# A narrow attention layer prepared by the layer ahead of it, and narrow layers that project one batch before their first scores

## What is computed

```python
x = x + tanh(g_xattn[0]) * L0_xattn(layernorm(x), ctx_768, ...)     # L0x: 16 heads of 8, biases, clipped scores
x = x + tanh(g_ffn[0])   * L0_ffn(layernorm(x), ...)                # butterfly transforms; weights "L0w"
...                                                                # L1x, L1f, L2x: heads of 64, experts
x = x + tanh(g_ffn[2])   * L2_ffn(layernorm(x), ...)                # L2f: ends in (y - mu) * rsqrt(var) * ln_g + ln_b
x = x + tanh(g_xattn[3]) * L3_xattn(layernorm(x), ctx_768, mask, Wq, Wk, Wv, Wo)   # L3x: no biases, a key mask
x = x + tanh(g_ffn[3])   * L3_ffn(layernorm(x), ...)

def attention(x, context):          # per batch b of 8, per head h of 16
    q, k, v = x @ Wq, context @ Wk, context @ Wv      # x: 256x128, context: 512x96
    p = softmax(q_h @ k_h.T * 8 ** -0.5)              # 256x512
    return concat_h(p @ v_h) @ Wo
```

## Time and profile before

| | |
|---|---|
| median of three runs | 1991.5 us (1983.24 to 1994.39) |
| the profiled execution's own time | 1993.19 us |
| its span, first to last instruction | 1991.4 us |
| L0x, block start to first row scores | 14.7 to 38.5 us |
| L0x, first exponential | 56.4 us |
| L2f ends, L3x begins | 1589.8, 1590.05 us |
| L3x, first row scores | 1614.6 us |
| L3x, first exponential | 1628.4 us |

### The profile page before, as it was taken

How to read it: one execution, slowest core, us unless ns; L and a number is a source line. 1 busy time by engine, 2 the same in 40 slices (tenths; PEclk the granted TensorE clock), 3 DMA queues, 4 the chain that set the end, 5 groups by cost and what they waited for, 6 DMA issues and landing times. The chain is left out here.

```text
span 1991.4 us, 42094 instructions
## 1 busy us (share of the span) xinstructions
PE 1743.8 (88%) x16392; PEld 1016.1 (51%) x16392; DVE 1283.0 (64%) x2318; ACT 1014.8 (51%) x1944; POOL 1062.2 (53%) x1436
## 2 busy tenths in 40 slices
PE   6899988969999999967957999999987799999335
PEld 2344333636666666645743666666654434444323
DVE  4899996566766666625446567666634558886571
ACT  1555544426666666645534666666652337766101
POOL 2388981127777787754034788888884021110026
PEclk9899999869999999988987999999997899999557
DMA  6411100300111111107010011111010022220302
GB/s 185 188 41 43 49 25 1 79 23 2 27 27 27 27 27 23 23 7 219 24 34 13 3 26 27 27 27 27 23 23 17 8 76 63 59 53 10 89 14 29
DMA packets 95687, 85.45 MB, mean 43 GB/s; under 512 B 13382, under 2 KB 85186, under 8 KB 95461
## 3 DMA queue, kind: packets, MB, share of 16 engines
q1 hardware_dynamic: 88481, 68.48, 13.3%
q10 hardware_dynamic: 3172, 10.10, 1.3%
q0 software_dynamic: 3840, 4.20, 1.2%
HBM read 65.74 MB, written 17.54 MB: 42 GB/s over the span
## 5 line engine op out<-in xcount | busy, mean ns | idle before, releaser
L1150 DVE TENSOR_REDUCE L2x_neg_max<-L2x_row_ps 128x2 f32<-128x1024 f32 x128 | 156.6, 1223 | 123.8 <-PE L2x_row_ps L976 123.6
L1150 DVE TENSOR_REDUCE L1x_neg_max<-L1x_row_ps 128x2 f32<-128x1016 f32 x128 | 155.6, 1216 | 121.4 <-PE L1x_row_ps L976 121.2
L757 POOL TENSOR_TENSOR L1x_fold<-L1x_probs 128x512 f32<-128x512 f32 x128 | 172.1, 1344 | 72.4 <-ACT L1x_probs L844 66.4
L363 ACT ACTIVATE L0x_probs<-L0x_st_ps 128x512 f32<-128x512 f32 x256 | 139.0, 595 | 130.0 <-PE L0x_st_ps L438 111.0
L757 POOL TENSOR_TENSOR L2x_fold<-L2x_probs 128x512 f32<-128x512 f32 x128 | 171.0, 1336 | 62.1 <-ACT L2x_probs L844 54.5
L844 ACT ACTIVATE L1x_probs<-L1x_st_ps 128x512 f32<-128x512 f32 x256 | 139.0, 595 | 93.2 <-PE L1x_st_ps L990 84.2
L844 ACT ACTIVATE L2x_probs<-L2x_st_ps 128x512 f32<-128x512 f32 x256 | 139.0, 595 | 92.9 <-PE L2x_st_ps L990 83.0
L363 ACT ACTIVATE L3x_probs<-L3x_st_ps 128x512 f32<-128x512 f32 x256 | 139.2, 597 | 63.2 <-PE L3x_st_ps L438 63.1
L562 DVE TENSOR_REDUCE L3x_neg_max<-L3x_row_ps 128x2 f32<-128x1024 f32 x128 | 155.4, 1219 | 19.0 <-PE L3x_row_ps L427 18.3
L562 DVE TENSOR_REDUCE L0x_neg_max<-L0x_row_ps 128x2 f32<-128x1024 f32 x128 | 155.0, 1214 | 12.7 <-PE L0x_row_ps L427 11.9
L1008 PE MATMUL L1x_u_ps<-L1x_probs,L1x_vst 128*64 128x256 f32 x1024 | 124.6, 385 | 1.2 <-ACT L1x_probs L844 1.2
(11 more groups left out here) (629 smaller groups left out, 4773.5 us busy)
## 6 DMA issues: line engine op xcount, KB each, us to landing
L1x_r_wide<-scratch_r SPq DMA_DIRECT2D x14, 512.0 KB, 6.7
L2x_r_wide<-scratch_r SPq DMA_DIRECT2D x14, 512.0 KB, 6.3
L0w_up<-in_L_ffn_up_weights ACTq DMA_DIRECT2D x9, 512.0 KB
L0w_down<-in_L_ffn_down_weights ACTq DMA_DIRECT2D x9, 512.0 KB
L0x_kst<-scratch_L0x_k SPq DMA_DIRECT2D x8, 512.0 KB, 4.1
L3x_kst<-scratch_L3x_k SPq DMA_DIRECT2D x8, 512.0 KB, 4.2
scratch_L0x_k<-L0x_k_hi SPq DMA_DIRECT2D x16, 128.0 KB, 2.3
L0x_qst<-scratch_L0x_q SPq DMA_DIRECT2D x8, 256.0 KB, 2.7
```

The costliest lines, as they stand in the source:

```text
L363: act.activation(probs[n % PROBS][:, 2 * half:2 * half + 2, :], st_ps[half][:, :, :], ACT.Exp, scale=sh.scale).then_inc(exp_ready, 1)
L757: pool.tensor_tensor(fold[:, :, :], pr[:, 0:2, :], pr[:, 2:4, :], ALU.add).then_inc(fold_step, 1)
L1150: dve.tensor_reduce(neg_max[k % 4][:, t, r % 2, :], row_ps[:, :, 0:sh.keys], AXX, ALU.max, negate=True)\
```

## The change

Two things are done.

For L3x, a new object `NarrowAhead` holds its weights, the contexts of batches 0 and 1 and its statistics in SBUF, outside both layers. L2f's SyncE stream issues the loads behind its own; L2f's VectorE computes statistics of tiles 0 to 3 in the middle of its last loop and ScalarE their two activations at the end; L2f's TensorE adds 24 filling products at its end. In L3x the seven loads, the 24 filling products and the wait for `preset` on TensorE go; GpSimd normalises batch 0 ahead of zeroing `vst` and batch 1 after it; the statistics of the other 12 tiles and their activations move behind the opening's takes.

For both narrow layers, the opening makes only K, XT and Q of batch 0, with 16 filling products behind Q. V of batch 0 and XT, K, Q and V of batch 1 become bank users of steps -10 to -6. SyncE writes K and Q before it loads either of them (`write_k`, `write_q`, `load_k`, `load_q`). L0x's ScalarE still calls `folding.load` directly behind the opening's takes, which are now three instead of eight.

```diff
+LEAD_USES = {-10: [("V", 0)], -9: [("XT", 1)], -8: [("K", 1)], -7: [("Q", 1)], -6: [("V", 1)]}
...
     def bank_uses(self, n):
...
-        out = []
+        out = LEAD_USES.get(n, [])[:]
...
     def opening(self):
-        return [("K", 0), ("XT", 0), ("Q", 0), ("XT", 1), ("V", 0), ("K", 1), ("Q", 1), ("V", 1)]
+        return [("K", 0), ("XT", 0), ("Q", 0)]
...
+class NarrowAhead:
+    tiles = 2 * QT
...
+    def issue(self, sp):
+        for dst, src in self.loads:
+            sp.dma_start(dst, src).then_inc(self.loaded, 16)
+        for p in range(2):
+            sp.dma_start(self.ctxb[p][0:DC, :], self.ctxT[p]).then_inc(self.ctx_loaded[p], 16)
...
-            load_ctx(0)
-            for dst, src in loads:
-                sp.dma_start(dst, src).then_inc(loaded, 16)
-            load_ctx(1)
-            stack_k(0)
-            stack_q(0)
-            stack_k(1)
-            stack_q(1)
+            if not ahead:
+                load_ctx(0)
+                for dst, src in loads:
+                    sp.dma_start(dst, src).then_inc(loaded, 16)
+                load_ctx(1)
+            for p in range(2):
+                write_k(p)
+                write_q(p)
+                load_k(p)
+                load_q(p)
...
             folded = rows_done = 0
+            if ahead:
+                normalise(0)
             for v in vst:
                 ins = pool.memset(v[:, :, :, :], 0.0)
...
             pool.wait_ge(preset, 2)
+            if ahead:
+                normalise(1)
             pool.wait_ge(rstd_ready, 2)
-            normalise(0)
-            normalise(1)
+            if not ahead:
+                normalise(0)
+                normalise(1)
...
-            act.wait_ge(stats_ready, 2)
-            act.activation(lnv[:, :], mv[:, :, 1], ACT.Ln, bias=eps[:, 0:1]).then_inc(rstd_ready, 1)
-            act.wait_ge(rstd_ready, 1)
-            act.activation(rstd[:, :], lnv[:, :], ACT.Exp, scale=-0.5).then_inc(rstd_ready, 1)
-            act.wait_ge(preset, 2)
+            if not ahead:
+                scales()
+            if not sh.bias:
+                act.wait_ge(bias_ready, 1)
             for key in sh.opening():
                 take(key)
+            if ahead:
+                scales()
+            act.wait_ge(preset, 2)
             if folding:
                 folding.load(act)
...
             keep_busy(1, sh.opening_fill[0])
             pe.wait_ge(loaded, 16 * len(loads))
-            pe.wait_ge(preset, 2)
-            for key in sh.opening():
+            if sh.bias:
+                pe.wait_ge(preset, 2)
+            for at, key in enumerate(sh.opening()):
                 use(key)
-                keep_busy(1, sh.opening_fill[1])
+                keep_busy(1, sh.opening_fill[1 + at])
...
             dve.wait_ge(loaded, 16 * len(loads))
             for key in sh.opening():
                 if key[0] in ("Q", "K"):
                     take(key)
+            if ahead:
+                statistics()
...
+                ahead.issue(sp)
...
                         down(k, i)
+                pe.wait_ge(hid_ready, 4 * chunks)
+                keep_busy(24)
...
+                act.wait_ge(next_rows, 3)
+                act.activation(ahead.lnv[:, first], ahead.mv[:, first, 1], ACT.Ln, bias=eps[:, 0:1]).then_inc(next_rstd, 1)
+                act.wait_ge(next_rstd, 1)
+                act.activation(ahead.rstd[:, first], ahead.lnv[:, first], ACT.Exp, scale=-0.5)
...
+                    if t == ahead.tiles - 1:
+                        ins.then_inc(next_rows, 1)
+                        dve.wait_ge(next_rows, 1)
+                        for i in range(ahead.tiles):
+                            ins = dve.bn_stats(ahead.stats[:, i, :], x_res[:, i, :])
+                        ins.then_inc(next_rows, 1)
+                        dve.wait_ge(next_rows, 2)
+                        for i in range(ahead.tiles):
+                            ins = dve.bn_aggr(ahead.mv[:, i, :], ahead.stats[:, i, :])
+                        ins.then_inc(next_rows, 1)
...
                 narrow_attention(nc, Narrow("L0x", clip=True, bias=True, mask=False, out_bias=True, gate=0,
-                                             opening_fill=(24, 6), lead_fill=2, step_fill=2, fill_always=True),
+                                             opening_fill=(24, 6, 6, 16), lead_fill=2, step_fill=2, fill_always=True),
...
             narrow_attention(nc, Narrow("L3x", clip=False, bias=False, mask=True, out_bias=False, gate=3,
-                                         opening_fill=(24, 6), lead_fill=3, step_fill=1, fill_always=False),
+                                         opening_fill=(0, 6, 6, 16), lead_fill=3, step_fill=1, fill_always=False),
```

More of the change, by code:

```diff
@@ L128, in dve_caps, with __init__, sb, narrow_attention @@
         return True
-def narrow_attention(nc, sh, dram, res, const, folding=None):
+class NarrowAhead:
+    tiles = 2 * QT
+    def __init__(self, nc, ctx, name, dram):
+        def sb(n, shape, dt=F32):
+            return ctx.enter_context(nc.sbuf_tensor(f"{name}_{n}", shape, dt, side="right"))
+        _, _, sem = alloc(nc, ctx, name)
+        self.wq, self.wk, self.wv, self.wo = sb("wq", [P, D]), sb("wk", [P, D]), sb("wv", [P, D]), sb("wo", [P, 2, D])
+        self.sel, self.ctxb = sb("sel", [P, HEADS]), [sb(f"ctxb{i}", [P, SK]) for i in range(2)]
+        self.stats, self.mv = sb("stats", [P, NT, 6]), sb("mv", [P, NT, 2])
+        self.lnv, self.rstd = sb("lnv", [P, NT]), sb("rstd", [P, NT])
+        self.loaded, self.ctx_loaded = sem("loaded"), [sem(f"ctx_loaded{i}") for i in range(2)]
+        self.loads = [(self.wk[0:DC, :], dram["Wk"]), (self.wv[0:DC, :], dram["Wv"]), (self.wq[:, :], dram["Wq"]),
+                      (self.wo[:, :, :], dram["Wo_rows"]), (self.sel[:, :], dram["sel"])]
+        self.ctxT = dram["ctxT"]
+    def issue(self, sp):
[3 more added lines that the diff above has]
+            sp.dma_start(self.ctxb[p][0:DC, :], self.ctxT[p]).then_inc(self.ctx_loaded[p], 16)
+def narrow_attention(nc, sh, dram, res, const, folding=None, ahead=None):
     x_res, gates, after = res
@@ L139, in narrow_attention @@
         sb, ps, sem = alloc(nc, ctx, sh.name)
-        wq, wk, wv = sb("wq", [P, D]), sb("wk", [P, D]), sb("wv", [P, D])
-        wo = sb("wo", [P, 2, D])
         bq = sb("bq", [P, 1])
         bo = sb("bo", [1, D]) if sh.out_bias else None
[L144 to L147, removed]
+        if ahead:
+            wq, wk, wv, wo, sel, ctxb = ahead.wq, ahead.wk, ahead.wv, ahead.wo, ahead.sel, ahead.ctxb
+            stats, mv, lnv, rstd = ahead.stats, ahead.mv, ahead.lnv, ahead.rstd
+        else:
+            wq, wk, wv = sb("wq", [P, D]), sb("wk", [P, D]), sb("wv", [P, D])
+            wo = sb("wo", [P, 2, D])
+            sel = sb("sel", [P, HEADS])
+            ctxb = [sb(f"ctxb{i}", [P, SK]) for i in range(2)]
+            stats, mv = sb("stats", [P, NT, 6]), sb("mv", [P, NT, 2])
+            lnv, rstd = sb("lnv", [P, NT]), sb("rstd", [P, NT])
+        tiles = range(ahead.tiles if ahead else 0, NT)
+        rest = slice(tiles.start, NT)
         xn, xnT = sb("xn", [P, QT, D]), sb("xnT", [P, SQ])
@@ L164, in narrow_attention @@
         bank = ps("bank", [P, 512])
-        loaded, preset, stats_ready, rstd_ready = sem("loaded"), sem("preset"), sem("stats_ready"), sem("rstd_ready")
-        zeroed = sem("zeroed")
-        ctx_loaded, xn_ready = [sem(f"ctx_loaded{i}") for i in range(2)], sem("xn_ready")
+        preset, stats_ready, rstd_ready = sem("preset"), sem("stats_ready"), sem("rstd_ready")
+        zeroed, bias_ready = sem("zeroed"), sem("bias_ready")
+        if ahead:
+            loaded, ctx_loaded = ahead.loaded, ahead.ctx_loaded
+        else:
+            loaded, ctx_loaded = sem("loaded"), [sem(f"ctx_loaded{i}") for i in range(2)]
+        xn_ready = sem("xn_ready")
         bank_full, bank_free = sem("bank_full"), sem("bank_free")
@@ L319, in _, with scales @@
         def _(act):
+            def scales():
+                act.wait_ge(stats_ready, 2)
+                act.activation(lnv[:, rest], mv[:, rest, 1], ACT.Ln, bias=eps[:, 0:1]).then_inc(rstd_ready, 1)
+                act.wait_ge(rstd_ready, 1)
+                act.activation(rstd[:, rest], lnv[:, rest], ACT.Exp, scale=-0.5).then_inc(rstd_ready, 1)
             def take(key):
@@ L540, in _ @@
             else:
-                dve.memset(bq[:, :], 0.0)
+                dve.memset(bq[:, :], 0.0).then_inc(bias_ready, 1)
             for part in shift_parts:
@@ L544, in _, with statistics @@
             ins.then_inc(preset, 1)
[L545 to L551, removed]
+            def statistics():
+                for t in tiles:
+                    ins = dve.bn_stats(stats[:, t, :], x_res[:, t, :])
+                ins.then_inc(stats_ready, 1)
+                dve.wait_ge(stats_ready, 1)
+                for t in tiles:
+                    ins = dve.bn_aggr(mv[:, t, :], stats[:, t, :])
+                ins.then_inc(stats_ready, 1)
```

(9 more changed lines are left out.)

24 lines of the change are left out of this document (17 added, 7 removed).

## The result

The changed kernel takes 2015.1 us (median; 2012.8 to 2024.4) against 1993.0 us of the kernel before in the same runs: a ratio of 1.0127, 95% interval 1.0102 to 1.0152. It is slower by 22 us by the two medians and by 25 by the ratio, outside the range of 1986 to 2007. Its profiled execution has a span of 2013.4 us, 22.0 above the one before.

The account below looks back on a forecast made before the run. The first exponentials of L0x and L3x were taken to move the end one for one, L0x's set by ScalarE's queue. L0x +7.8 and L3x -2.2 summed to +5.6 us, taken as 1998.0, range 1986.0 to 2007.0.

Parts of the forecast that it names:

- the price of the clock: Both narrow layers' leads: time lost to TensorE's half clock, +4.0 us in L0x and +2.3 in L3x.
- part (d): L3x's lead: idle TensorE drops the clock for one to three steps, +2.3 us, ends 0 and +4.
- L2f's end: Last loop of L2f: VectorE's added statistics and waits make the block end later, +1.45 us.
- L3x, block to row scores: L3x's opening: row scores come 14.4 us after the block opens; -8.7 us with L2f's later end included.
- The bank uses in the lead: L3x's lead: V, XT, K, Q and V between steps lengthen it, +4.2 us, from +2.9 to +5.4.
- ScalarE's issuing: L0x: the 24 weight loads occupy ScalarE's queue for 19.5 us, from 26.5 to 46.0.
- Rival 1: L0x: ScalarE's issues are short when started early, 10.8 us for 24; total 1986; chance 8%.
- What L0x waited for at 46: L0x: the lead stands still until ScalarE is free at 46.0, with XT of batch 1 waiting at step -9.
- Rival 2: L0x: Q's load of batch 0 is starved by the weight loads; L0x +13, total +11, 2004 us; chance 22%.
- the early row scores gain only two heads: L0x's lead: two heads' row scores run early, then XT's wait for ScalarE stops it until 46.0.
- I take the shift as kept: L0x and L3x: a shift of the first exponential moves the end one for one.
- the upper end: Upper part of the forecast range, counted with the starved Q load in the 0.25 for slower by over 0.5%.

Follow-up runs that it names:

- e1_l0_old: Changed kernel with L0x's opening of before (eight bank uses, then the weight loads), L3x as changed; 1998.4 us against 1991.5 before, ratio 1.0039.
- e3_l3_fill: e1_l0_old with 36 instead of 16 filling products behind Q in L3x; 1987.1 us, ratio to the kernel before 0.9982.
- e4_l0_fill: Changed kernel with 90 instead of 16 filling products behind Q in L0x; 2007.3 us, ratio to the kernel before 1.0111.
- e7_one_a_step: e3_l3_fill with L0x's 24 weight loads issued one a step in steps -10 to 13; 1982.0 us against 1991.1 before, ratio 0.9950.
- e9_l3_no_lead_fill: e1_l0_old without the three filling products of each step before step 4 in L3x; 2016.8 us, ratio to the kernel before 1.0124.
- e2_ahead_only: e1_l0_old with L3x's opening of before too, keeping only the preparation inside L2f and SyncE's new order; ratio to the kernel before 1.0021.
- e10_l0_lead3: e7_one_a_step with three instead of two filling products a step in L0x's lead; 1983.2 us against 1995.0 before, ratio 0.9950.
- e11_both_lead3: e8_both_short with three filling products a step in L0x's lead; ratio to the kernel before 0.9976.
- e8_both_short: Changed kernel, 36 fills behind Q in both layers, L0x's loads two a step in steps -5 to -1, one in 0 to 13; ratio 0.9976.
- e5_loads_behind: Changed kernel with L0x's 24 weight loads issued behind V of batch 1 (step -6) instead of Q of batch 0; ratio to the kernel before 1.0086.
- e12_l3_fill26: e1_l0_old with 26 instead of 16 filling products behind Q in L3x; one execution, 1986.6 us.

## Why the prediction was wrong

The step that failed is the price of the clock, twice. In L3x, part (d), it was +2.3 with ends 0 and +4; e1_l0_old against e3_l3_fill shows 31.6 - 17.7 = 13.9 us. In L0x it was +4.0, at most 6.5; e4_l0_fill shows 10.5. Each time the fall itself was forecast, from rows 6 and 11. Two sizes were off. The low stretch was taken from rows 6, 10 us, and in L3x as one to three steps; it lasted 51 us in L0x and 34 in L3x, all of the lead. The warning stood in rows 6: TensorE was busy from 58 us and the clock rose only at 65.7. I had read these 8 us as busy and still low, and did not carry them over to a lead of the same row scores and fills. And a step at half clock takes 1.93 us with two fills and 2.36 with three, not 1.7 and 2.1. These two terms, 6.3 us in the forecast and 24.4 measured, are 18.1 of the 20.4 us by which the two layers came out above their +5.6.

The other terms, one by one:
- L2f's end: +1.45 forecast; the updates with the statistics between them take 5.6 us instead of 4.3, +1.3. Right.
- L3x, block to row scores: 14.4 forecast, 14.3 measured, 14.2 to 16.1 in the experiments with this opening. K ran at half clock (1.77 us) as said. Right.
- The bank uses in the lead: +4.2 forecast. With the clock up, L3x needs 17.3 instead of 13.4 us (+3.9) in e3_l3_fill, and L0x 16.1 instead of 12.3 (+3.8) in e4_l0_fill. Right.
- ScalarE's issuing: 26.5 to 46 forecast, 26.75 to 45.66 measured. The Trainium skill's "usually small relative to the DMA itself" ("DMA: Bandwidth & Descriptors", section "Issuing engines are not separate DMA queues") did not hold here: 18.9 us of ScalarE. Where the issues were spread it is borne out, 0.33 us each in e7_one_a_step. Rival 1, short issues because they start early, fell.
- What L0x waited for at 46: forecast was ScalarE, with XT waiting at step -9; it was Q's load, with row score 0. Rival 2 had this, by 10 us for the writes (7.0 measured), a landing of 9.5 (11.2 measured) and a total of 47.1 (row scores at 46.1). The two waits ended within half a microsecond of each other, ScalarE's at 45.66, so the forecast of 46.0 was near by luck. The step "the early row scores gain only two heads" failed with it: they gained none, and heads -10 and -9 and V were still to do at 46.1. From the first row scores to step 0 that takes 16.1 us at full clock (e4_l0_fill), to 62.2 instead of the forecast's 60.0: these 2.2 us and the clock's 6.5 are most of the 9.3 us by which L0x's first exponential missed. That taking away the loads' traffic alone would have gained no more than two heads, because XT would then have waited for ScalarE, follows from the order of the code and wasn't tried by itself.
- The sum: L0x +7.8 forecast, +17.1 at the first exponential and +18.2 at the last; L3x -2.2 forecast, +7.6 from the block's opening to the first exponential, with the 1.3 of L2f's end +8.9.
- "I take the shift as kept" held for the narrow layers, within 3 us. But 7 us come back in between. In the profiled executions the stretch from L0x's last exponential to L2f's last update took 1245 to 1259 us, 1251.6 before and 1245.7 in the changed kernel, though L2f's end is 1.3 us longer there. The clock was low for 166 us of it before and for 143 in the changed kernel, with the same code up to L2f's last loop; why is not shown. This is the size of the spread within any of these kernels, and luck as far as the total goes: without it the miss would have been larger.

The chances put 0.25 on slower by over 0.5%, for rival 2 and the upper end. Rival 2's mechanism came true, at a higher price: it gave L0x +13 us, with two steps and V of batch 0 counted "at low clock (5.5 us)", and +17.1 were measured, with every step of the lead at half clock.

## What to carry to other kernels

Moving work off TensorE's path makes a hole, and the hole can cost more than the work: where a chain of scores starts behind a transfer, fill the time up to its landing (20 products more were worth 11 us), and price a fallen clock at every product until a row of similar work shows it back up, not at one or two steps. A burst of large transfers can hold the engine that issues it (18.9 us here) and delay small transfers of others (11.2 us instead of 3.8); issue it behind the small ones that others wait for, and spread it. And look at the same stretch in every profile at hand before a cause is given to a fallen clock: one execution with it up is not yet a remedy. Before a list of early work is shortened, look at what stands behind it on each engine: here 24 loads moved up with it.

## What the hardware showed unexpectedly

- A low clock can last 85 us in which TensorE counts as busy for 97%: 1602.3 to 1687.6 us in e9_l3_no_lead_fill, with row scores (float16, 32 rows) and the bank's float32 products in the lead, and the heads' products behind it. With three dense products of 128 rows a step added to the lead it lasted 34.1 us, in four profiles.
- The clock can fall within a busy stretch, and not in every execution of the same work: at 43.8 us in e7_one_a_step and at 43.1 in e2_ahead_only, two dense products a step, busy for 1.75 of 2 us ahead of it, but in none of five other profiles with the same lead. With three a step it stayed up in the profiles of e10_l0_lead3 and e11_both_lead3; it also stayed up with two in e4_l0_fill and e8_both_short. That the third product matters is not shown.
- It fell 2.1 us after TensorE's last product ahead of L0x's lead (the changed kernel and e5_loads_behind) and 3.7 to 4.6 us after it ahead of L3x's, and did not fall in an idle time of 1.87 us (e12_l3_fill26).
- Q's load of 256 KB took 2.7 us in the kernel before and 3.8 in e5_loads_behind, without weight loads beside it, and 11.2 us beside them in the changed kernel, while the DMA engines moved 408 to 420 GB/s (36 to 46 us).
